# Queries and keys packed into three column blocks, scores on four row groups, with a reordered layer body, routing loads and final stage

## The reference, cut to what matters

```
z = layernorm(x)
q, k, v = z@wq+bq, z@wk+bk, z@wv+bv            # 8 heads of 48 features
s = q_h @ k_h.T * 48**-0.5 + adj               # per graph and head, 128x128
ctx = softmax(s) @ v_h
y = rmsnorm(z + ctx@wo + bo)
x = x + rmsnorm(y + silu(y@w1+b1) @ w2 + b2)   # w1 384x1536, w2 1536x384

xg = l2norm(layernorm(x)) * gamma_in           # per graph, 128 x 384
logits1 = xg @ phi.T                           # 128 slots = 8 experts x 16
disp1, comb1 = softmax over nodes, softmax over slots
yn = l2norm(disp1.T @ xg)                      # 128 slot rows per graph
# second routing, per outer expert k: logits2 = yn_k @ l2norm(mean(yn_k) @ w_slot2[k]).T
slots2 = softmax over slots of logits2, applied to yn
o = 32 experts: (v * gelu(gate)) @ w2[k,e],  [v, gate] = slots2 @ w1[k,e]    # hidden 1024
out = x + comb1 @ (comb2 @ o)
```

## Time and profile before

| | |
|---|---|
| median of 3 runs | 3154.0 us (3153.85 to 3154.65) |
| the profiled execution | 3154.5 us, of which its span (first to last instruction) 3152.7 us |
| busy: TensorE / its weight loads / VectorE / ScalarE / GpSimd | 93% / 90% / 60% / 49% / 47% |
| mean granted TensorE clock | 0.972 of full speed |
| set-up | 0 to 45 us |
| the layer | 45 to 1860 us |
| dispatch | 1860 to 2230 us |
| experts | 2230 to 3066 us |
| combine | 3066 to 3153 us |

### The profile page before, as it was taken

The page is one execution under the profiler, slowest core; times in us unless marked ns, Lnnn a source line. Parts: engine busy times, 40 slices in busy tenths (PEclk is TensorE's granted clock), DMA queues, the critical chain, the costliest instruction groups (busy, mean ns, idle before and its releaser), DMA issues. The chain is left out here.

```text
span 3152.7 us, 62729 instructions
## 1 busy us (share of the span) xinstructions
PE 2925.6 (93%) x21523; PEld 2822.0 (90%) x21523; DVE 1877.5 (60%) x3053; ACT 1535.9 (49%) x3982; POOL 1472.6 (47%) x1486
## 2 busy tenths in 40 slices
PE   3999999999999999999999857788799999999986
PEld 2999999999999999999999847788799999999982
DVE  4465656565665656565665525555577777777754
ACT  3354554545454554545454425555545545544530
POOL 0344444343444444343444424444377677677650
PEclk9899999999999999999999968899899999999999
DMA  4010101010010101010110133432566666666869
GB/s 127 13 41 25 45 25 45 25 45 23 33 36 25 45 25 45 25 45 23 35 35 25 34 95 115 120 118 75 176 210 208 209 210 213 205 212 205 265 224 367
DMA packets 289913, 320.82 MB, mean 102 GB/s; under 512 B 23688, under 2 KB 289416, under 8 KB 289800
## 3 DMA queue, kind: packets, MB, share of 16 engines
q1 hardware_dynamic: 281128, 307.17, 31.2%
q10 hardware_dynamic: 8704, 12.58, 1.1%
HBM read 260.97 MB, written 58.72 MB: 101 GB/s over the span
## 5 line engine op out<-in xcount | busy, mean ns | idle before, releaser
L1531 PE MATMUL u_bank<-x_in,x_w 128*128 128x256 f32 x4608 | 574.5, 283 | 5.7 <-DVE x_w L1619 5.7
L1531 PEld LDWEIGHTS u_bank<-x_in,x_w 128*128 128x128 f32 x4608 | 569.6, 192 | 5.8 <-issue 5.8
L927 POOL TENSOR_TENSOR hT_lo<-h_tmp,hT_hi 128x512 fp32r<-128x512 f32 x192 | 248.0, 1292 | 432.0 <-DVE hT_hi L815 432.0
L1688 POOL TENSOR_TENSOR x_aT<-x_act,x_aT 128x512 fp32r<-128x512 f32 x128 | 299.6, 2341 | 182.1 <-ACT x_aT L1596 182.1
L388 PE MATMUL m_bank<-yT_hi,w_hi 128*128 128x256 f32 x1152 | 339.7, 295 | 0.0
L388 PE MATMUL m_bank<-yT_lo,w_hi 128*128 128x256 f32 x1152 | 324.4, 282 | 0.0
L388 PE MATMUL m_bank<-yT_hi,w_lo 128*128 128x256 f32 x1152 | 323.7, 281 | 0.0
L1684 POOL TENSOR_TENSOR x_w<-raw,x_w 128x768 fp32r<-128x768 f32 x128 | 274.2, 2142 | 102.4 <-DVE x_w L1627 102.4
L661 ACT ACTIVATE h_tmp<-m_bank,b1c 128x256 f32<-128x256 f32 x384 | 160.9, 470 | 329.8 <-PE m_bank L388 329.4
L1587 ACT ACTIVATE x_gelu<-u_bank,x_b1T 128x256 f32<-128x256 f32 x256 | 121.9, 476 | 409.8 <-PE u_bank L1531 409.8
L1543 PE MATMUL o_bank<-x_w,x_aT 128*128 128x384 f32 x1536 | 287.8, 335 | 1.8 <-POOL x_aT L1688 1.8
(11 more groups left out here) (214 smaller groups left out, 7307.6 us busy)
## 6 DMA issues: line engine op xcount, KB each, us to landing
raw<-in_L_ffn_w_dram SPq DMA_DIRECT2D x384, 384.0 KB, 4.7
ws_raw<-in_L_ffn_w_slot_dram SPq DMA_DIRECT2D x32, 576.0 KB, 5.0
x_in<-in_x_dram SPq DMA_DIRECT2D x32, 384.0 KB, 3.4
x_res<-in_x_dram SPq DMA_DIRECT2D x32, 384.0 KB, 4.1
residual<-f_sb SPq DMA_DIRECT2D x32, 384.0 KB, 2.5
yn<-yn_sb SPq DMA_DIRECT2D x32, 384.0 KB, 2.5
expert_out<-x_o SPq DMA_DIRECT2D x64, 192.0 KB, 3.0
c_o<-expert_out SPq DMA_DIRECT2D x32, 384.0 KB, 5.8
```

The lines of the kernel that those rows point to most:

```text
L927: nc.gpsimd.tensor_tensor(hT[i % 3][1][:], h_tmp[i % 2][:], hT[i % 3][0][:].bitcast(F32), ALU.subtract).then_inc(hl.sem, 1)
L1531: mm = pe.matmul(u_bank[n % BANKS][:, g, :], w1s[i % 2][a][:, c, g, c2 * P:(c2 + 1) * P], xT[e % 2][b][:, c, :], start=c == 0 and j == 0, ...
L1688: nc.gpsimd.tensor_tensor(aTs[i % 2][1][:], aT[i % 2][:], aTs[i % 2][0][:].bitcast(F32), ALU.subtract).then_inc(al.sem, 1)
```

## The change

- wq and wk are no longer padded. A permutation of their columns (`by_head_parts`) puts the first 32 features of the 8 heads into blocks 0 and 1 (four heads each), and the last 16 features of all 8 heads into block 2. q and k have three blocks each. Block 2 of q is written twice, each time with half of its features multiplied by zero (`half_scale`, `half_bias`).
- The scores of one graph become 16 products of 32 rows by 128 columns on four row groups: for each head one product of its first 32 features and one of block 2, added up in PSUM. Row group i writes bank i, and the fourth bank is the one that was `r_bank`. Scores of both graphs follow each other; they wait for `v_ok` of both graphs and for the slots of the first routing.
- The hand-written orders of PE, ScalarE and VectorE in the layer's body change.
- In dispatch, `load_ws(t,1)` is issued after the first four loads of rows and ahead of `load_cb`, `store_ct(d,1)` and four more loads of rows; ScalarE does `ws_high(t,1)` behind the last `turn`.
- `combT` gets another layout in memory, is loaded as a whole into the space of the experts' raw weights during the last expert, and the last residual tiles go into `slots2T` there too. combine loads only `c_o`, and its rounds are written out.

```diff
-    wq_s = split_pair("wq", [P, DC, H * HP])
-    wk_s = split_pair("wk", [P, DC, H * HP])
+    wq_s = split_pair("wq", [P, DC, D])
+    wk_s = split_pair("wk", [P, DC, D])
...
+def by_head_parts(flat, parts):
+    copies = []
+    by_head = flat.rearrange("p (c h e) -> p c h e", c=DC, h=H)
+    first = [x[:, :, 0:2 * P].rearrange("p c (h i) -> p c h i", i=HG) for x in parts]
+    copies.append([by_head[:, :, :, 0:HG], *first])
+    for a in range(2):
+        last = [x[:, :, 2 * P:D].rearrange("p c (g b i) -> p b c g i", b=2, i=DH - HG)[:, a] for x in parts]
+        copies.append([by_head[:, :, 4 * a:4 * a + 4, HG:DH], *last])
+    return copies
...  set-up, small loads
-                sp.wait_ge(zeroed.sem, 3)
-                    for half in range(2):
-                        src = b.rearrange("(m two e) -> two e m", two=2, e=DH)[half]
-                        for m in range(H // 2):
-                            small_load(sp, bqk[HP * half:HP * half + DH, n, m:m + 1], src[:, m:m + 1])
+                    for h in range(H):
+                        m, g = divmod(h, 4)
+                        small_load(sp, bqk[HG * g:HG * g + HG, n, m:m + 1], column[h, 0:HG])
+                        last = HG * g + (DH - HG) * m
+                        small_load(sp, bqk[last:last + DH - HG, n, 2:3], column[h, HG:DH])
...  PE
+            def scores(g, t, r):
+                if t == 0:
+                    pe.wait_ge(q_ok.sem, q_ok.at(g, 4))
+                    pe.wait_ge(k_ok.sem, k_ok.at(g, 3))
+                    pe.wait_ge(v_ok.sem, v_ok.at(g, 2))
+                    if r is not None and past(r, 1):
+                        pe.wait_ge(sl_ok.sem, sl_ok.at(r - 1, 2))
+                for m in range(2):
+                    for q, k in ((m, m), (2 + m, 2)):
+                        for i in range(4):
+                            rows = slice(HG * i, HG * i + HG)
+                            mm = pe.matmul(banks[:, i, t * GN + m * P:t * GN + (m + 1) * P], qT[rows, q, tok(t)],
+                                           kT[rows, k, tok(t)], start=k < 2, stop=k == 2)
+                mm.then_inc(a_full.sem, 1)
...  PE, the body
-                if A: project(a, U_Q, wq_s, 0); project(a, U_Q, wq_s, 1)
+                if A: project(a, U_Q, wq_s, 0)
                 if M: up(m, 0)
-                if A: project(a, U_K, wk_s, 0); project(a, U_K, wk_s, 1)
+                if A: project(a, U_Q, wq_s, 1); project(a, U_K, wk_s, 0)
                 if M: up(m, 1)
-                if A: values(a, 0); values(a, 1); scores(a, 0)
-                if R: xnT_step(r, 0)
-                if M: down(m, 0)
-                if A: scores(a, 1)
-                if R: xnT_step(r, 1)
+                if A: project(a, U_K, wk_s, 1); values(a, 0); values(a, 1); scores(a, 0, r); scores(a, 1, r)
+                if M: down(m, 0); up(m, 2)
                 if A: prob_T(a, 0)
-                if R: logits(r)
-                if A: context(a, 0)
-                if M: down(m, 1)
-                if A: prob_T(a, 1)
+                if R: xnT_step(r, 0, a)
+                if M: down(m, 1)
+                if A: context(a, 0)
+                if R: xnT_step(r, 1, a)
+                if A: prob_T(a, 1)
+                if R: logits(r)
+                if M: up(m, 3)
                 if R: logits_T(r)
-                if M: up(m, 2)
-                if A: context_T(a, 0); context(a, 1)
-                if M: up(m, 3)
-                if A: project_out(a, 0); context_T(a, 1)
+                if A: context_T(a, 0); context(a, 1); project_out(a, 0); context_T(a, 1)
...  ScalarE, the body
+                if A: exps(a, 0); exps(a, 1)
                 if R: xnT_step(r, 0)
-                if A: exps(a, 0)
+                if A: prob_T(a, 0)
                 if R: xnT_step(r, 1)
-                if A: prob_T(a, 0); exps(a, 1)
+                if A: prob_T(a, 1)
...  VectorE, scores(g, t)
+                dve.wait_ge(a_full.sem, a_full.at(g, U_S[1] + 1))
...  dispatch, SyncE and ScalarE
                 if O and T and t < E1 - 1: load_yn(t + 1, 0, 1, 2, 3)
+                if T and R: load_ws(t, 1)
                 if O and R: load_cb(d + 1, 1)
                 if O: store_ct(d, 1)
                 if O and T and t < E1 - 1: load_yn(t + 1, 4, 5, 6, 7)
-                if T and R: load_ws(t, 1)
...
-                means(t, 0); turn(t, 4); turn(t, 5); ws_high(t, 1); turn(t, 6); turn(t, 7)
+                means(t, 0); turn(t, 4); turn(t, 5); turn(t, 6); turn(t, 7); ws_high(t, 1)
...  experts, the end of SyncE's block
+            for i in range(PIECES):
+                sp.wait_ge(w1_lo.sem, w1_lo.at(NX - 1, i + 1))
+                sp.dma_start(raw[:, i * RAW1:(i + 1) * RAW1], ct_of[:, i * RAW1:(i + 1) * RAW1]).then_inc(ct_landed.sem, 16)
+                if i == 1:
+                    sp.wait_ge(xl.sem, xl.at(NX - 1, 1))
+                    sp.dma_start(early[:, EARLY:NB, :], res_dram[EARLY * P:NB * P, :].rearrange("(g p) d -> p g d", p=P)
+                                 ).then_inc(res_landed.sem, 16)
+            sp.wait_ge(w2_lo.sem, w2_lo.at(NX - 1, PIECES))
+            sp.dma_start(raw[:, PIECES * RAW1:n_ct], ct_of[:, PIECES * RAW1:n_ct]).then_inc(ct_landed.sem, 16)
             for e in (E2 - 2, E2 - 1):
                 store(NX - E2 + e, E1 - 1, e)
...  combine, SyncE
-                sp.dma_start(ct[i][:], ct_dram[bass.ds(r * ROUND + i * G, G)].rearrange("g p n -> p g n")).then_inc(landed[i].sem, 16)
```

More of the change, by code:

```diff
@@ L207, in _ @@
             def _(act):
-                for i, (_, flat, parts) in enumerate(weights):
-                    act.wait_ge(staged[i].sem, 16 * len(weights[i][0]))
-                    nc.scalar.copy(parts[0], flat).then_inc(hi_done.sem, 1)
+                for i, (_, copies) in enumerate(weights):
+                    act.wait_ge(staged[i].sem, 16)
+                    for src, hi, _ in copies:
+                        nc.scalar.copy(hi, src).then_inc(hi_done.sem, 1)
                 act.wait_ge(small.sem, n_small[0])
@@ L247, in _ @@
                 pe.wait_ge(pool_done.sem, 5)
-                pe.wait_ge(lo_done.sem, len(weights) + 1)
+                pe.wait_ge(lo_done.sem, sum(len(copies) for _, copies in weights) + 1)
                 for c in range(DC):
@@ L410, in project @@
                 bank = A_BANK[uses[n]]
-                for half in range(2):
-                    m = 2 * n + half
-                    mm = split_mm(bank[:, half * GN:(half + 1) * GN],
+                for m in ((0, 1), (2,))[n]:
+                    mm = split_mm(bank[:, (m % 2) * GN:(m % 2 + 1) * GN],
                                   [[w[s][:, c, tok(m)] for s in range(2)] for c in range(DC)],
@@ L1698, in _, with combine @@
             over_experts(pool, body)
-def combine(nc, ctx, sb, ps, sem, ct_dram, o_dram, res_dram, out, early, res_landed):
+def combine(nc, ctx, sb, ps, sem, o_dram, out, early, res_landed, raw, ct_landed):
     G = 2
@@ L1720, in loop @@
             body(0, i)
-        with eng.Fori(1, EARLY // ROUND) as r:
-            for i in range(BUF):
-                body(r, i)
-        for r in range(EARLY // ROUND, ROUNDS):
+        for r in range(1, ROUNDS):
             for i in range(BUF):
@@ L1751, in body @@
                         pe.wait_ge(added.sem, added.at(r - 1, G * i + g + 1))
-                    pe.matmul(bank[i][g][:, 0:D], ct[i][:, g, :], o_sb[i][:, g, :], start=True, stop=True).then_inc(full.sem, 1)
+                    pe.matmul(bank[i][g][:, 0:D], raw[:, (r * ROUND + i * G + g) * P:(r * ROUND + i * G + g + 1) * P], o_sb[i][:, g, :], start=True, stop=True).then_inc(full.sem, 1)
             loop(pe, body)
```

220 lines of the change are left out of this document (106 added, 114 removed).

## The result

The changed kernel takes 3167.9 us (median of 6 runs, 3165.6 to 3174.5), the kernel before beside it 3153.6 us (6 runs, 3151.8 to 3154.7). The ratio is 1.0048 with a 95% interval of 1.0036 to 1.0061: slower by half a per cent, where I had forecast 3054 us. The profiled execution took 3169.1 us, its span 3167.3.

What follows compares the result with a forecast made beforehand. Layer bound by TensorE's matmul count and spacing, dispatch by TensorE's waits for ScalarE, combine by data movement. Layer -40, dispatch -48, combine -15, set-up +3 sum to -100 us from 3154.5: 3054 us, range 3032 to 3115.

Steps and rivals of the forecast that it cites:

- Products and mode of the scores: Layer, per group: 18 fewer projection matmuls, -2.16 us; scores mode entered once, -0.29; 64 score records take 1.79 us.
- two overlap: Rival, scores: only two row groups run side by side, +1.79 us per group, +57 in all, 3111 us; chance 0.09.
- partial overlap: Rival, scores: a slot of four records takes 0.140 us instead of 0.112, +14 us, 3068 us; chance 0.14.
- none overlap: Rival, scores: 32-row products run singly, +172 us, 3226 us; chance 0.10, shared with a new wait of that size.
- The wait ahead of prob_T, -0.4: Layer: TensorE's wait of 0.4 us per group in front of prob_T disappears.
- New waits 1 and 2: Layer, TensorE per group: 0.8 us before scores for both graphs' v_ok, 0.8 before context for ScalarE's exponentials and copies.
- The remaining reorderings ... I cost them at nothing: Layer: other order changes cost nothing; if slack is gone, up(4) is late and 0.5 us per group lost.
- The clock in the layer: Slow TensorE clock after waits was counted in dispatch only, where removing it was worth 11.8 us.
- the -3 that I expected where TensorE waits for xn: Layer's last body with up and down: down(0) and up(2) fill 4.3 us of the wait before xnT_step, -3 us.
- I expect nothing there apart from its end: Experts: no matmul changed, so no change except late loads at the end, costing 0 to 1 us.
- dispatch and combine: dispatch: -48 us from 38.5 us of waits and 11.8 of slow clock; combine: -15 us from 5.8 MB moved earlier.
- Set-up: Before the layer: wq and wk loads 5 us sooner, 16 more small loads +7.4 to +9.8; +3 us.

Runs made afterwards that it cites:

- silu_first: Changed kernel plus 32 do-nothing TensorE instructions (3132.8 us), with ScalarE's silu(5) ahead of the slots' square and GpSimd's h_lo(5) ahead of the slots' power: 3100.4 us.
- exps_split: Changed kernel plus 32 do-nothing TensorE instructions (3132.8 us), with ScalarE copying out prob_T(0) and xnT before the second graph's exponentials: 3080.9 us.
- down_before_scores: Changed kernel plus 32 do-nothing TensorE instructions (3132.8 us), with down(m,0) ahead of the scores on TensorE: 3191.1 us.
- tail_alone: Kernel before with only the changed combine, one raw tensor, the combT layout and the loads in the last expert; old layer and dispatch: 3137.4 us.
- all_waits_moved: Changed kernel plus 32 do-nothing instructions; silu(5), h_lo(5) earlier, second exponentials later, down(m,0) before scores, down(m,1) and up(m,3) before prob_T(a,0) and prob_T(a,1): 3053.0 us.
- dispatch_and_tail: Kernel before with the dispatch reorderings and the tail change (combine, raw tensor, combT, late loads), keeping the old layer and set-up: 3087.7 us.

## Why the prediction was wrong

*Products and mode of the scores: right.* 18 fewer projection matmuls, -2.16; one entry instead of two, -0.29; four groups side by side, 2.00 us for 64 records. The rivals "two overlap", "partial overlap" and "none overlap", 0.33 of my chances, are all answered by that one row. The Trainium skill's factor of 3.07 (TensorE: Matmul & The Clock Gate, "Measured speedup vs the span model"; it is given for 512 columns), weighed in the prediction, would have made the products alone 2.33 us. The row has 2.00 with the entry, 7.17 / 2.00 = 3.6 times, and the measurement decides.

*The wait ahead of prob_T, -0.4: right in the loop.* The list of TensorE's waits has it twice in the whole layer (4.2 us), where it had it 33 times (8.8 us). By that list it was 0.27 us a group, less than the 0.4 of the weight loads.

*New waits 1 and 2: right in place and cause, a little small.* The gaps between records are 1.18 us (1002.68 to 1003.86) and 1.16 (1013.45 to 1014.61) where a matmul needs 0.17: 1.0 us each, for 0.8. That is 12 us in all.

*"The remaining reorderings ... I cost them at nothing": this step failed.* I gave the chain behind `project_out` "the same matmuls beside it as now" and let up(4) be what it might delay. The chain is late, because GpSimd gets two hT_lo late and has them ahead of it. But it is down(5) that pays, through VectorE's slot rows, ScalarE's square and silu(5), and GpSimd's hT_lo: a gap of 1.72 us where there would be 0.17 (34 times, 38.4 us by the waits). `silu_first` takes that wait away with one swap on two engines.

*The clock in the layer: missing from the sum.* I had it as a cost of dispatch's waits alone, and the layer got two new waits of the same kind, if shorter. It is worth 15 us. `exps_split` removes it with the wait for pT; `down_before_scores` makes it worse.

Per group: -2.16 - 0.29 - 0.4 + 1.0 + 1.0 + 1.55 = +0.70, with 8 x 1.68 / 29 = 0.46 for the clock +1.16; measured 0.58 and 0.46, +1.04. Times 29 groups that is 30 of the stage's 36.7 us. The bodies ahead of and behind the loop make up the rest, which I did not take apart; the -3 that I expected where TensorE waits for xn did not come, the two waits there were 17.3 us before and are 9.8 and 7.3 (the last is labelled "issue").

*Experts: "I expect nothing there apart from its end": this step failed,* by 38.1 us, and for a reason that none of my rivals had. The loop's code is fetched again in each turn because of where it stands: 22.4 us of waits at its head, 2.4 of another and some 13 for the half clock behind them. The instruction queue was on the profile's page that I read, 49 packets; I did not ask what it would do when TensorE's code moves.

*dispatch and combine: right.* -45.0 in the traces and -47.8 alone for -48 (a step takes 33.9 us for my 33.2). The 38.5 us of waits went as I said; the clock gave back about 6 us where I had 11.8. Combine has -16.0 and -16.8 for -15. The tail's late loads cost the experts nothing that `tail_alone` shows.

*Set-up: +0.8 for +3.* The two opposite terms were of the right kind; which of them was smaller was not tried.

With the order mended and the code in a good place the same change is worth about what the sum promised: `all_waits_moved` at 0.9674 against `dispatch_and_tail` at 0.9783, the old layer with the same rest, is 35 us less for the new layer and set-up, where the forecast had -37. That agreement is in part luck. The forecast reached 53.3 us a group with two waits of 0.8 in it; this kernel has neither, and by the terms that are left it should take 54.52 - 2.85 = 51.7 us, and takes 53.1. Of the 1.4 us, 0.8 are the two waits that surfaced (14.8 and 10.0 us over some 31 groups); the rest is open.

## What to carry to other kernels

When a change moves work on one engine, walk the queue of every engine that shares a stage with it, and ask of each instruction what its neighbour ahead waits for; a term "costs nothing" needs the name of that neighbour. Removing a wait is worth its length only if TensorE has other work up to the next producer: the same swap of down(m,0) costs 58 us alone and is part of the fastest kernel with two more moves. And when an unchanged loop of well over a thousand instructions becomes slower with its waits labelled "issue", compare the packets of the instruction queue and the length of the jump back before looking for a cause in the data; some do-nothing instructions ahead of the loop are the test, and a cure for as long as nothing else moves the code.

## What the runs showed of the hardware

- A loop of 1611 TensorE instructions runs without a fetch, or with 41 packets of 16 KB between 2440 and 2950 us, a jump back of 3.7 to 6.6 us in place of 0.2 and some 7.6 us more in each turn, by where it stands. Up to the first jump back 10850 instructions give no stall, 10955, 10967 and 10971 do, 10987 and 11050 do not.
- A wait that is already met is not free on TensorE: 22.5 us for 200 instructions that hold two such waits each, 0.11 us per instruction.
- 32-row products on four row groups with a bank each run side by side: 64 records in 2.00 us, where 32 records of 48 rows took 2 x 1.09.
- With gaps of 1.0, 1.0 and 1.55 us in each group TensorE had a stretch of 3.4 us at 1.2 GHz in every third or fourth group. Without the one ahead of the 48-column matmuls of `context` it had none from 120 to 1690 us, though the two others stayed (`exps_split`); without the one of 1.55 the stretches stayed, six of them (`silu_first`). Why the one decides was not tried.
